# Attention stage: a later wait for the stacks, two large loads issued in slot 1, and the last value pieces spread over two steps

## The reference, cut to what matters

```python
q = hidden_states @ Wq.T
k = hidden_states @ Wk.T
v = hidden_states @ Wv.T
...
q_rope = _apply_rope(q_rope, cos, sin)
k_rope = _apply_rope(k_rope, cos, sin)
scores = jnp.einsum('bqhd,bkhd->bhqk', q_nope, k_nope) / math.sqrt(DN) + jnp.einsum('bqhd,bkhd->bhqk', q_rope, k_rope) / math.sqrt(DR)
attn = jax.nn.softmax(scores, axis=-1)
out = jnp.einsum('bhqk,bkhd->bqhd', attn, v)
out = out.reshape(B, S, H * DV)
return out @ Wo.T
```

## Time and profile before

| | |
|---|---|
| median of 3 runs | 671.05 us (670.73 to 671.31) |
| the profiled execution's own time | 671.69 us |
| its span | 669.9 us |
| PE busy | 656.0 us (98%) |
| DVE, ACT, POOL busy | 66%, 61%, 37% of the span |
| attention | from 0 to about 401 us |
| mean granted clock of PE | 0.997 of full speed |

### The profile page before, as it was taken

One profiled execution on the slowest core, in us unless ns is written; L12 is line 12 of the kernel. 1 busy time (PEld: TensorE's weight loads), 2 busy tenths in 40 slices (PEclk: granted clock), 3 DMA queues, 4 the chain that ended last, 5 costly groups with the idle time before them and its releaser, 6 DMA issues. The chain is left out here.

```text
span 669.9 us, 15243 instructions
## 1 busy us (share of the span) xinstructions
PE 656.0 (98%) x5297; PEld 630.9 (94%) x5297; DVE 438.9 (66%) x952; ACT 410.5 (61%) x1085; POOL 245.9 (37%) x279
## 2 busy tenths in 40 slices
PE   9999999999999999999999999999999999999995
PEld 8989999999999999999999899999996799999995
DVE  6566557557666755765665577556559986556877
ACT  5556667666776666866577774334689964333553
POOL 3731863134353133632328454212361462222011
PEclk9999999999999999999999999999999999999998
DMA  7174655436543435544363404100166200000000
GB/s 254 39 226 139 202 170 145 135 100 174 163 133 111 126 123 170 163 137 118 96 186 120 111 1 151 32 0 0 41 202 246 76 1 1 1 1 0 1 33 31
DMA packets 38172, 69.74 MB, mean 104 GB/s; under 512 B 3440, under 2 KB 22640, under 8 KB 37872
## 3 DMA queue, kind: packets, MB, share of 16 engines
q1 hardware_dynamic: 37696, 68.38, 33.7%
q10 hardware_dynamic: 432, 0.79, 0.4%
HBM read 52.18 MB, written 16.97 MB: 103 GB/s over the span
## 5 line engine op out<-in xcount | busy, mean ns | idle before, releaser
L312 PE MATMUL PJ<-xTh,WBh 128*128 128x256 f32 x364 | 106.8, 293 | 0.1
L314 PE MATMUL PJ<-xTh,WBl 128*128 128x256 f32 x364 | 103.0, 283 | 0.0
L313 PE MATMUL PJ<-xTl,WBh 128*128 128x256 f32 x364 | 102.8, 282 | 0.0
L851 POOL TENSOR_TENSOR stage<-stage 128x256 f32<-128x256 f32 x32 | 24.4, 764 | 162.4 <-DVE stage L718 162.4
L611 ACT ACTIVATE probs<-probs,rinv 128x256 f32<-128x256 f32 x128 | 58.4, 508 | 26.3 <-DVE rinv L734 26.3
L312 PEld LDWEIGHTS PJ<-xTh,WBh 128*128 128x128 f32 x364 | 69.6, 191 | 0.9 <-DVE Vl L723 0.3
L313 PEld LDWEIGHTS PJ<-xTl,WBh 128*128 128x128 f32 x364 | 69.6, 191 | 0.0
L314 PEld LDWEIGHTS PJ<-xTh,WBl 128*128 128x128 f32 x364 | 69.4, 191 | 0.0
L723 DVE TENSOR_TENSOR QKl<-PJ,QKh 128x512 fp32r<-128x512 f32 x63 | 43.4, 689 | 37.2 <-ACT QKh L599 37.0
L866 POOL TENSOR_TENSOR WBl<-raw,WBh 128x512 fp32r<-128x512 f32 x32 | 40.8, 1294 | 30.7 <-ACT WBh L628 30.7
L1091 POOL TENSOR_SCALAR vare<-mv 128x2 f32<-128x2 f32 x13 | 2.9, 223 | 132.1 <-DVE mv L1084 132.1
(11 more groups left out here) (340 smaller groups left out, 2516.1 us busy)
## 6 DMA issues: line engine op xcount, KB each, us to landing
K<-scr_k SPq DMA_DIRECT2D x60, 256.0 KB, 4.4
raw<-in_w_att SPq DMA_DIRECT2D x37, 256.0 KB, 4.8
Q<-scr_q SPq DMA_DIRECT2D x15, 512.0 KB, 7.3
stage<-scr_m SPq DMA_DIRECT2D x6, 768.0 KB, 4.0
scr_q<-rot_h SPq DMA_DIRECT2D x30, 128.0 KB
scr_q<-rot_l SPq DMA_DIRECT2D x30, 128.0 KB
scr_k<-rot_h SPq DMA_DIRECT2D x30, 128.0 KB
scr_k<-rot_l SPq DMA_DIRECT2D x30, 128.0 KB
```

Source lines behind the costliest of these rows:

```text
L312: pe.matmul(out, ah, bh, start=(i == 0), stop=False)
L313: pe.matmul(out, ah, bl, start=False, stop=False)
L314: last = pe.matmul(out, al, bh, start=False, stop=(i == n - 1))
```

## The change

There are four edits.

1. In `scores`, a head at j = 0 (from slot 1 on) does the three products on QKh and QKl of both halves of the queries first, and waits for `stack_q` and `stack_k` only then, ahead of its four products with the stacks. The number of matmuls is the same.
2. On SP, had, w2t and xres (in this order) are no longer issued between fill(1) and spill(2), but in slot 1, behind the five raw pieces and ahead of spill(3). Nothing changes on POOL and DVE, which wait for these loads.
3. For slot 14 alone, `ORDER` is replaced by `LAST_ORDER`: value piece 6 of slot 15 is made in step 2 (before it was step 3) and value piece 7 in step 3 in the first place (before in the second).
4. ACT and DVE take the high and low halves of pieces 6 and 7 in the new places as well.

The last hunks, in which `ORDER[j]` becomes `order(k, j)` in the same way on PE, ACT and DVE, are left out after the first ones:

```diff
--- before.py
+++ after.py
@@ -170,11 +170,15 @@
 
 
         ORDER = [([2], [3]), ([4], [5]), ([], []), ([6], [7])]
+        LAST_ORDER = ([2], [3]), ([4], [5]), ([], [6]), ([7], [])
         ROPE_STEP = 2
         EARLY_MAX = (0, 1, 2)
         ACC_STEP = 1
         WARM = 22
         TAIL = [(0, 1), (2,), (3,), (4,)]
+
+        def order(k, j):
+            return (LAST_ORDER if k == 14 else ORDER)[j]
 
         def w2_tile(i):
             return w2t[:, i, :] if i < FT else keep["stage"][:, 4 * PIECE:4 * PIECE + D]
@@ -263,8 +267,13 @@
             spill(1, 1, 0)
             spill(1, 1, 1)
             fill(1, 1)
-            sp.dma_start(xres[:, :, :], x_tok.rearrange("(t p) d -> p t d", p=P)).then_inc(res_in, 16)
-            sp.dma_start(had, had_d).then_inc(w2_in, 16)
+
+            def load_late():
+
+                sp.dma_start(had, had_d).then_inc(w2_in, 16)
+                sp.wait_ge(x_split, B)
+                sp.dma_start(w2t[:, :, :].rearrange("p (a b) d -> p a (b d)", b=2), w2_raw).then_inc(w2_in, 16)
+                sp.dma_start(xres[:, :, :], x_tok.rearrange("(t p) d -> p t d", p=P)).then_inc(res_in, 16)
 
             def emit(s, k, g):
 
@@ -287,14 +296,14 @@
                         sp.wait_ge(w_split, GP * (g + 1) + i - RING + 1)
                         sp.wait_ge(raw_in[i % RING], 48)
                         load(i)
+                if k == 1:
+                    load_late()
                 if k < 14:
                     spill(s + 2, k + 2, 0)
                     spill(s + 2, k + 2, 1)
                     fill(s + 2, k + 2)
 
 
-            sp.wait_ge(x_split, B)
-            sp.dma_start(w2t[:, :, :].rearrange("p (a b) d -> p a (b d)", b=2), w2_raw).then_inc(w2_in, 16)
             for s in (0, 1):
                 emit(s, s, 0)
             with sp.Fori(0, NG - 2) as g:
@@ -395,9 +404,7 @@
 
             def scores(s, k, j):
                 u, par, bank = 4 * s + j, k % 2, SC[j % 2]
-                if j == 0 and k:
-                    pe.wait_ge(stack_q[par], 8 * (s + par))
-                    pe.wait_ge(stack_k[par], 32 * (s + par))
+                apart = not k or j == 0
                 if j == 0 and not k:
                     pe.wait_ge(rope_lo, 2)
                 pe.wait_ge(part_split, 6 * s + j + 1)
@@ -406,16 +413,25 @@
                 for t in range(TT):
                     q, keys = slice(t * P, (t + 1) * P), slice(S, 2 * S)
                     out = bank[:, t, :]
-                    both = t > 0 and not k
+                    both = t > 0 and apart
                     pe.matmul(out, QKh[:, par, j, q], QKh[:, par, j, keys], start=not both, stop=False,
                               skip_group_check=both)
                     pe.matmul(out, QKh[:, par, j, q], QKl[:, par, j, keys], start=False, stop=False,
                               skip_group_check=both)
                     pe.matmul(out, QKl[:, par, j, q], QKh[:, par, j, keys], start=False, stop=False,
                               skip_group_check=both)
-                    if k:
+                    if not apart:
                         pe.matmul(out, Q2[:, par, j, q], K2[:, par, j, :], start=False, stop=False)
                         last = pe.matmul(out, Q2[:, par, j, q], K3[:, par, j, :], start=False, stop=True)
+                if apart and k:
+                    pe.wait_ge(stack_q[par], 8 * (s + par))
+                    pe.wait_ge(stack_k[par], 32 * (s + par))
+                    for t in range(TT):
+                        q, out = slice(t * P, (t + 1) * P), bank[:, t, :]
+                        pe.matmul(out, Q2[:, par, j, q], K2[:, par, j, :], start=False, stop=False,
+                                  skip_group_check=t > 0)
+                        last = pe.matmul(out, Q2[:, par, j, q], K3[:, par, j, :], start=False, stop=True,
+                                         skip_group_check=t > 0)
                 if not k:
                     r = slice(32 * j, 32 * j + 32)
                     for t in range(TT):
@@ -504,14 +520,14 @@
                     if j == ROPE_STEP and k < 14:
                         rope_piece(s + 2, k + 2, 0)
                     if k < 15:
-                        for p in ORDER[j][0]:
+                        for p in order(k, j)[0]:
                             piece(s + 1, k + 1, p)
                     if k > 0 or j >= 1:
                         turn_probs(u - 1, (j - 1) % 4, first=(k == 0 and j == 1))
                     if j == ROPE_STEP and k < 14:
                         rope_piece(s + 2, k + 2, 1)
                     if k < 15:
-                        for p in ORDER[j][1]:
+                        for p in order(k, j)[1]:
                             piece(s + 1, k + 1, p)
                     if j == 3 and k > 0:
                         output(s - 1, k - 1, first=(k == 1))
...
```

## The result

The changed kernel takes **677.68 us** (median of 6 runs, 677.03 to 685.63), the kernel before beside it on the same chip 671.18 (6 runs, 670.26 to 672.62). The ratio is 1.0118, 95% interval 1.0071 to 1.0164: 1.2% slower, 6.5 us where 2.5 were forecast, and outside the range. The profiled execution took 677.88, its span is 676.0 (before 669.9): 6.1 more. One of the six executions, that of 685.63, ran at a mean granted clock of 0.975, the others at 0.988 to 0.993.

A forecast was written before the change was run, and what follows sets the result against it. The prediction took PE, busy 98% of the span, as the bound. +1.3 us up to slot 3 and +1.2 from slot 14 gave +2.5 on the median of 671.05: 673.5 us, range 670.2 to 675.2.

The forecast's parts named there:

- the sum of +2.5: Whole kernel: +1.3 us up to slot 3 plus +1.2 us from slot 14 on, making it slower.
- when does w2t land: Slot 2: w2t lands at 72.6, by the pace of K and raw loads, so POOL waits 2.8 us.
- A: Up to slot 3: PE waits for POOL's weight splits, net of gains and absorption, +1.3 us, from 0 to +3.4.
- The Trainium skill's rate: Loads at slot 2: 435 GB/s over 16 ports would land K, raw and w2t by 66.8, ahead of POOL.
- Term B: Slot 14, step 2: piece 6 waits 2.75 us for its bank; net +1.2 us, from +0.65 to +1.64.
- the 0.45 that slot 15 was to absorb: Slot 15: PE's 0.30 wait for probs and its start-up would take back some 0.45 us of slot 14's loss.
- the main case: Whole kernel: both stalls come as forecast, 673.5 us, own range 672.2 to 675.8, chance 0.52.
- what the edits gain: Starts of slots 1 and 2: edits 1 and 2 remove waits of 0.73 and 0.88, PE 1.61 us earlier.
- The absorption at slot 3: Start of slot 3: a late PE finds its waits of 0.16 and 0.28 covered, taking 0.44 us off the loss.
- w2t in time: Rival at slot 2: loads run near full rate, POOL does not wait, sum +1.2, 672.3 us; chance 0.17.
- the gain at the end: Rival at slot 3: raw piece 5 lands early, w2t in time, sum -0.85, 670.2 us; chance 0.10.
- piece 6 without its wait: Rival in slot 14: DVE splits piece 5 early, edit 3 gives -1.1, 671.25 us; chance 0.08.

The follow-up runs named there:

- second trace of before: The unchanged kernel before, run and profiled once more: 670.71 us, ratio 0.9996, span 668.3.
- old order: Changed kernel with slot 14 in its former order (edits 3 and 4 undone): 674.69 us, ratio 1.0057.
- covered: Changed kernel with 22 useless matmuls ahead of value piece 6 in slot 14: 676.09 us, ratio 1.0079.
- N = 8: Changed kernel with edit 2 undone, plus 8 useless matmuls ahead of the first scores of slots 4, 8 and 12 each: 676.92 us, ratio 1.0086.
- loads back: Changed kernel with edit 2 undone, so xres, had and w2t stand ahead of spill(2) again: 671.11 us, ratio 1.0015.
- N = 22: Changed kernel with edit 2 undone, plus 22 useless matmuls ahead of the first scores of slots 4, 8 and 12 each: 679.17 us, ratio 1.011.
- N = 15: Changed kernel with edit 2 undone, plus 15 useless matmuls ahead of the first scores of slots 4, 8 and 12 each: 676.56 us, ratio 1.0088.
- w2t ahead of the raw pieces: Edits 1 and 2 with slot 14's former order; had and w2t issued before slot 1's five raw pieces, xres behind them: 671.76 us, ratio 1.0023.
- the two with 44 useless matmuls and loads back: Changed kernel, edit 2 undone, 44 useless matmuls in slot 14: ahead of head 58's scores 675.83 us, at the slot's start 680.06 us.
- the stall shifted: Changed kernel with edit 2 undone, 44 useless matmuls ahead of head 58's scores in slot 14, step 2: 675.83 us, ratio 1.0071.
- the banks swapped: Edits 1, 3 and 4 without edit 2; slot 15's value piece 6 in PJ1 and piece 7 in PJ0: 669.69 us, ratio 0.9991.
- xres late: Kernel with the banks swapped, and xres alone moved into slot 1 behind the raw pieces: 669.54 us, ratio 0.9991.
- POOL's sums early: Kernel with the banks swapped, and POOL's first nine w2 sums moved between its slots 0 and 1: 669.61 us, ratio 0.9989.

## Why the prediction was wrong

Sign, places and the causes of both stalls were right; the sum of +2.5 was 3.6 short of the 6.1 between the profiled executions. The step that failed is the price of a stall: the sum counts it as its length alone and puts the granted clock behind it at nothing. The runs show a stretch at half clock behind each, 1.6 and 1.5 us. Against the second trace of before (span 668.3) the difference is 7.7, and the sum 5.2 short.

- **What shows the steps.** PE's waits at slots 1 and 2 went; POOL was released by w2t's DMA; PE waited for POOL's WBl at 81.2; piece 6 waited 2.69 for DVE's QKl and OTl's wait went. The places and releasers are as stated, the sizes not all: POOL started at 73.65 and not at 72 to 73, PE waited 4.5 and not about 3, and ACT's wait for raw piece 5 shrank from 5.37 to 1.09, because ACT itself came later.
- **Step "when does w2t land": 73.6, not 72.6.** The K fill and the issues came as reckoned: K's last part, issued at 60.97, landed 5.0 later, at 66.0 (forecast 66.3). The raw pieces did not keep the pace: the last, issued at 63.71, took 7.1 us and landed at 70.8, 4.8 behind K and not 3.5. From there w2t took 2.8, as reckoned. The row of the last raw piece:

```profile
DMA to landing us min/median/max: 7.1/7.1/7.1
```

Why the raw pieces were slower than in the kernel before, where the last took 5.5, no run separates; in the program the difference is that had, w2t and xres are now issued right behind them. POOL's chain behind w2t was as forecast (12.12 from the first addition to the end of the splits, 12.19 forecast), so PE was 2.82 later than before and not 1.7: +1.1. Without the clock A would have stayed within its ends of 0 to 3.4 (3.87 - 1.6 = 2.3); with it A lies above them.
- **The Trainium skill's rate** (page "DMA: Bandwidth & Descriptors", "Where 436 GB/s comes from") had put w2t there at 66.8, as an estimate; it landed 6.8 us later. The page gives a ceiling of the ports, which a later landing does not contradict; as a pace for loads issued in a row it was too fast here. Going by the pace in the rows was the right choice.
- **No term for the clock.** The sum of A took a stall as lost time alone. Behind the 4.67 us of standing still PE ran at the lower level until about 90, 1.6 lost. With it A is 1.3 + 1.1 + 1.6 = 4.0, measured 3.87.
- **Term B: +2.4, not +1.2.** The stall was as forecast, and its own price 1.5 (old order 44.60, covered 46.09), within 0.65 to 1.64. The 0.45 that slot 15 was to absorb hardly showed: PE's wait for probs there is 0.27 with the stall and without it. Another 1.5 are the clock's. Of these 3.0 edit 1 takes 0.6 back, which the prediction had at nothing ("in the other slots ... nothing"), so that 2.4 show against before (45.19). The missing 3.6, then: clock 3.1, landing 1.1, B's stall 0.3, less 0.6 for edit 1 in the rest and 0.3 that the terms leave over (0.1 in A, 0.2 behind attention).
- **Two sums of the prediction do not come out of its own terms.** The low end of B is given as 0.65; 1.64 less 0.65 less 0.45 is 0.54. And the ends of A and B give 671.7 to 676.1 for the main case, not 672.2 to 675.8. Neither matters to the miss.
- **Step "what the edits gain": 1.61.** Of this 0.73 stood in the one execution shown and 0.13 in the next. Against the second trace of before A is 360.23 - 354.90 = 5.33: 4.67 - 0.91 (0.13 + 0.78) of standing still, and 1.6 of clock.
- **The absorption at slot 3** came as reckoned against the first trace: both waits there were covered. Against the second there was nothing to absorb.
- **Rivals.** w2t in time, the gain at the end, piece 6 without its wait: none came. xres landed at 76.3 (11.2 from its issue at 65.08), ahead of DVE's need at 79.9.

## What to carry to other kernels

Before a load is moved down a queue, find the engine that awaits it in program order and what stands behind it there; the slack here was 0.4 us, though w2 itself is used only behind attention. Work moved into a gap fills it only if its bank is free by then; giving the piece another bank took 2.7 us of waiting away. In a kernel that is bound by PE, price a new stall of some us at its length plus a slow stretch that may follow, here 1.5 to 1.6 us each; and read two executions of before, since waits of half a us come and go.

## What the runs showed of the hardware

- **A stall in a PE that is otherwise 98% busy can bring its clock down.** Behind 4.2 to 4.8 us of standing still near 81 to 86 the granted clock fell to 0.50 in all four traces that have it, and was back at 1.00 by 92; the price was 1.6 in the one worked out. Behind 2.7 it fell in four traces (both of the change, N = 8 and 15) and stayed in two (loads back, N = 22), and by their mean clock in two more executions with N = 15; behind 3.4 it fell in the one trace that has it. Behind the shorter waits in attention from 36 us on, 1.3 us and less, it stayed in every trace.
- **Useless matmuls during the wait keep it up**: 47.61 against 46.09, one pair of runs.
- **Behind attention the clock fell behind a wait of only 0.7 us, in some executions.** In four of the seventeen traces (w2t ahead of the raw pieces, the two with 44 useless matmuls and loads back, N = 8) the clock's row has an 8 in slice 32, where no edit is. All four fall 0.5 to 0.7 us behind the same wait of PE for DVE; with the stall shifted:

```profile
521.56 0.38 PE L1568 MATMUL UGP<-WI 32*128 32x256 f32 x2 [0.70 <-DVE rows L1928]
...
522.00:524.00 2.00, 2.00 (x20) 1.31 (x16) 1.32 (x4) 1.69 (x6) 1.61 (x1) 0.52 0.86 353
524.00:526.00 2.00, 2.00 (x13) 1.32 (x13) 1.97 (x5) 1.52 (x5) 0.00 (x0) 0.50 0.85 349
```

The other thirteen have the same wait (0.68 to 0.69) and stay at 1.00 there; whether the wait brings the fall about, no run tests. From the first UGP behind attention to the end of the program it takes 270.3 to 270.7 in the four and 268.2 to 268.6 in the others: 2 us. The ten executions of the kernel with loads back fall in two groups, six of 670.7 to 671.2 at a mean clock of 0.997 or more and four of 672.6 to 673.3 at 0.995 or less. That fits, but these four left no trace. Executions of one kernel thus differ by about 2 us, and the account above goes by stretches of the traces.
- **A gain at one wait reappears at the next.** Slot 14 started between 354.6 and 355.2 in the second trace of the kernel before, with edit 1 alone, with the loads back, with the banks swapped, with xres late and with POOL's sums early, wherever 0.1 to 0.8 us were lost or saved up to slot 3.
